# Two tile lists in one block: experts begin on the full tiles of 29 groups

## The reference

```
h = concat(tokens(x) * pos, txt)                        # 128 x 97 x 128
h = h + attn(layernorm(h))     # 8 heads, complex weights, decay mask, gate
h = h + ffn(layernorm(h))

# inside ffn, b*s = 12416 tokens:
o = softmax_attention(x) @ Wo + bo
t = layernorm(x + o) * ln1_g + ln1_b
probs = softmax(t @ gate_W + gate_b)
idx, gw = argmax(probs), max(probs)                     # one of E = 8 experts
hid = gelu(t @ W1[idx] + b1[idx])                       # 128 -> 512
out = (hid @ W2[idx] + b2[idx]) * gw                    # 512 -> 128
```

## Time and profile before

| | |
|---|---|
| median of 3 runs | 1433.87 us (1432.84 to 1434.1) |
| profiled execution | 1432.25 us, of it span 1430.4 |
| PE busy | 1341.3 us (94%), mean granted clock 0.974 |
| DVE busy | 1008.9 us (71%) |
| ACT busy | 723.4 us (51%) |
| POOL busy | 411.4 us (29%) |
| HBM | read 101.27 MB, written 20.82 MB |

### The profile page before, as it was taken

The page is one execution under the profiler, slowest core; times in us unless marked ns, Lnnn a source line. Parts: engine busy times, 40 slices in busy tenths (PEclk is TensorE's granted clock), DMA queues, the critical chain, the costliest instruction groups (busy, mean ns, idle before and its releaser), DMA issues. The chain is left out here.

```text
span 1430.4 us, 40339 instructions
## 1 busy us (share of the span) xinstructions
PE 1341.3 (94%) x14876; PEld 984.3 (69%) x14877; DVE 1008.9 (71%) x2308; ACT 723.4 (51%) x1630; POOL 411.4 (29%) x268
## 2 busy tenths in 40 slices
PE   6889999999999999999999999999999861999996
PEld 5457666666666666666666666666665550999996
DVE  1477777777777777777777777777778643566664
ACT  2135555555555555555555555555555451556654
POOL 0000222222222222222222222222222224466665
PEclk9999999999999999999999999999999895999999
DMA  7522322232222222322233333333310002333331
GB/s 296 216 73 72 83 83 82 83 83 83 83 83 83 83 83 82 83 83 83 83 86 89 93 88 86 88 95 84 85 42 15 18 14 54 104 104 102 102 100 53
DMA packets 94839, 124.57 MB, mean 87 GB/s; under 512 B 56587, under 2 KB 77117, under 8 KB 94176
## 3 DMA queue, kind: packets, MB, share of 16 engines
q1 hardware_dynamic: 38112, 102.47, 22.7%
q0 software_dynamic: 56576, 19.93, 6.7%
HBM read 101.27 MB, written 20.82 MB: 85 GB/s over the span
## 5 line engine op out<-in xcount | busy, mean ns | idle before, releaser
L1126 POOL DMA_INDIRECT expert_rows<-row_sb,placei x128 | 275.7, 2154 | 618.9 <-DVE z L922 566.9
L359 PE MATMUL bank_emb<-x_sb,wtok 128*128 128x256 f32 (+1 forms) x1216 | 323.5, 393 | 4.4 <-DMA x_sb<-in_x_main 3.4
L359 PEld LDWEIGHTS bank_emb<-x_sb,wtok 128*128 128x128 f32 (+1 forms) x1216 | 220.8, 191 | 104.0 <-issue 50.8
L862 DVE TENSOR_TENSOR sm<-bank_s,con 97x776 f32<-97x776 f32 x256 | 240.1, 959 | 26.1 <-PE bank_s L413 13.8
L876 DVE TENSOR_REDUCE mx<-bank_s 97x8 f32<-97x776 f32 x128 | 120.4, 961 | 57.9 <-PE bank_s L479 57.7
L1297 POOL DMA_INDIRECT out_tokens<-yo,tok x104 | 126.1, 1213 | 90.9 <-issue 55.0
L413 PE MATMUL bank_s<-qm,xn 32*97 32x452 f32 x1024 | 133.3, 583 | 4.3 <-DVE prob L881 2.2
L881 DVE TENSOR_TENSOR prob<-bank_s,mx 97x776 f32<-97x776 f32 x128 | 120.7, 964 | 3.3
L731 ACT ACTIVATE prob<-prob 97x776 f32<-97x776 f32 x128 | 108.4, 847 | 26.5 <-DVE prob L881 26.5
L1227 PE MATMUL bank_s<-w2e,hid 128*128 x832 | 109.7, 275 | 0.0
L869 DVE COPY vp<-bank_s 97x128 f32<-97x128 f32 x256 | 70.3, 286 | 55.6 <-PE bank_s L413 55.4
(11 more groups left out here) (181 smaller groups left out, 2330.1 us busy)
## 6 DMA issues: line engine op xcount, KB each, us to landing
x_sb<-in_x_main SPq DMA_DIRECT2D x96, 768.0 KB, 7.2
row<-expert_rows SPq DMA_DIRECT2D x104, 129.0 KB
w1e<-in_exp_w SPq DMA_DIRECT2D x1, 2576.0 KB, 11.7
txt<-in_txt_t SPq DMA_DIRECT2D x32, 64.0 KB, 2.3
w2e<-in_exp_w SPq DMA_DIRECT2D x1, 2048.0 KB, 16.9
expert_rows<-row_sb,placei POOLq DMA_INDIRECT x128, 7.9
out_tokens<-yo,tok POOLq DMA_INDIRECT x104, 2.5
x_sb<-in_x_tail SPq DMA_DIRECT2D x32, 48.0 KB, 2.5
```

Of the source, the lines that this page charges most:

```text
L359: mm = pe.matmul(banks["emb"][:, 0:NPG], wtok[0:k, c, :], x_sb[0:k, c, :], start=(c == 0), stop=(c == KC - 1))
L862: ins = dve.tensor_tensor(sm[:, k % 2, 2 * h:2 * h + 2, :], pair(h), decay, ALU.mult)
L1126: pool.indirect_dma_start(out=rows[:, :], out_offset=bass.IndirectOffsetOnAxis(ap=placei[:, k, c:c + 1], axis=0), in_=row_sb[:, k, c, E:E ...
```

## The change

There is one block instead of two. The list is made in two parts:

- The first has 80 tiles (`NT1`, turns 0 to 9). It is made from `run_k`, a copy of the counts after 29 groups (`KF`), by rounding down, so that it holds full tiles alone. DVE runs it at the end of round 31, PE's product and DVE's copy into `tab` come at the end of round 32. What each expert gave to it is kept in `taken`.
- The second has the other 24 tiles. DVE makes it from the final counts in small pieces, one after each slot of turns 0 and 1; PE's product (in bank s3) and the copy come after turn 1.

SP loads tiles as soon as the scatters of 29 groups have landed, x is used up and the first list is there. The eight blank stores stand between the loads of turns 2 and 3. Before tile 80 SP waits for all scatters, the blanks and the second list. POOL starts on the output scatters right after stage one's last. `w1b` and `row` lie where `x_sb` and `wtok` were (`home_x`), `hid`, `t_t` and `y` where `sm` and `prob` were (`home_s`). `run_i` is made inside `run_on` of the last group. PE waits for five banks to be drained and for the expert weights before its first tile. ACT has turn 0 written out and loops over the rest, PE and DVE have two loops. The steps of stage two (`tile_t`, `hidden`, `output`, `tile_in`, `result`) are unchanged. In the diff, `first_list` and `second_list` are cut to their ends; their middles are the chain of before, the second with `yield` between its steps.

```diff
+TURNS1 = 10
+NT1 = TURNS1 * SLOTS
+KF = next(k for k in range(NG) if -(-(k * N - E * (P - 1)) // P) >= NT1)
+LISTED = KF - 1 + 3 + 1
...
+        home_x = sb("home_x", [P, KC * NPG + KC * P])
+        home_s = sb("home_s", [P, 64 * S])
+
+        def view(home, a, d1, d2, n=P):
+            return home[0:n, a:a + d1 * d2].rearrange("p (a b) -> p a b", a=d1)
+
+        x_sb = view(home_x, 0, KC, NPG)
+        wtok = view(home_x, KC * NPG, KC, P)
+        w1b = view(home_x, 0, SLOTS, PACK)
+        row = view(home_x, SLOTS * PACK, SLOTS, ROW)
+        sm = home_s[0:S, 0:32 * S].rearrange("p (a b c) -> p a b c", a=2, b=4)
+        prob = home_s[0:S, 32 * S:64 * S].rearrange("p (a b c) -> p a b c", a=2, b=4)
+        hid = home_s[:, 0:SLOTS * FF].rearrange("p (s f n) -> p s f n", s=SLOTS, f=FB)
+        t_t = view(home_s, SLOTS * FF, SLOTS, P)
+        y = view(home_s, SLOTS * FF + SLOTS * P, SLOTS, P)
+        yo = sb("yo", [P, SLOTS, P])
+        tok = sb("tok", [P, SLOTS, 1], I32)
...
+        def scattered(eng, n):
+
+            for k in range(ROWS):
+                eng.wait_ge(s_scat[k], 16 * G * len(range(k, n, ROWS)))
...
+            def load(n, s):
+                if later(n):
+                    sp.wait_ge(s_yo, SLOTS * n + s + 1 - SLOTS)
+                first = sp.value_load(tab[0:1, 0, bass.ds(SLOTS * n + s, 1)], min_val=0, max_val=E * REG)
+                sp.dma_start(row[:, s, :], rows[bass.ds(first, P), :]).then_inc(s_row[s], 16)
+
+            def clear(e):
                 first = sp.value_load(run_i[0:1, e:e + 1], min_val=e * REG, max_val=e * REG + B * S)
                 sp.dma_start(rows[bass.ds(first, P), :], blank[:]).then_inc(s_blank, 16)
+
+            for k in range(4):
+                sp.wait_ge(s_xused[k], NG)
+            scattered(sp, KF)
+            sp.wait_ge(s_list, 1)
+            for s in range(SLOTS):
+                load(0, s)
+            for s in range(SLOTS):
+                load(1, s)
+            sp.wait_ge(s_run, 1)
+            for n in range(2, 4):
+                for s in range(SLOTS):
+                    load(n, s)
+                    if s % 2:
+                        clear((n - 2) * 4 + s // 2)
+            with sp.Fori(4, TURNS1) as n:
+                for s in range(SLOTS):
+                    load(n, s)
+            scattered(sp, NG)
+            sp.wait_ge(s_blankin, 32)
+            sp.wait_ge(s_blank, 16 * E)
+            sp.wait_ge(s_list, 2)
+            with sp.Fori(TURNS1, TURNS) as n:
+                for s in range(SLOTS):
+                    load(n, s)
+            for s in range(SLOTS):
+                sp.wait_ge(s_out[s], 16 * TURNS)
...
+            def first_list():
+                pe.wait_ge(s_tokens, NG)
+                pe.wait_ge(s_spread, 1)
+                pe.matmul(banks["emb"][:, 0:2 * NT1], const("ones"), spread[:, :, 0:NT1],
+                          start=True, stop=True).then_inc(s_tabm, 1)
+
+            def second_list():
+                free(pe, "s3")
+                pe.wait_ge(s_spread, 2)
+                pe.matmul(banks["s3"][:, 0:2 * (NT - NT1)], const("ones"), spread[:, :, NT1:NT],
+                          start=True, stop=True).then_inc(s_tabm, 1)
 
...
+                if i == LISTED:
+                    first_list()
...
+            pe.wait_ge(s_list, 1)
+            pe.wait_ge(s_ew, 32)
+            for bank in ("z", "x", "y", "s0", "s1"):
+                free(pe, bank)
+            tile_t(0, 0)
+            tile_t(0, 1)
+            hidden(0, 0)
+            turn(0)
+            turn(1)
+            second_list()
+            with pe.Fori(2, TURNS1) as n:
+                turn(n)
+            pe.wait_ge(s_list, 2)
+            with pe.Fori(TURNS1, TURNS - 1) as n:
+                turn(n)
+            turn(TURNS - 1, True)
 
 
...
+            act.preload_act_table(ACT.Gelu_apprx_tanh)
...
+                if g == KF:
+                    dve.wait_ge(s_runk, 1)
...
+                if g == KF - 1:
+                    read(dve, g, "C.rank")
+                    dve.tensor_copy(run_k[:], run[:]).then_inc(s_runk, 1)
+                if g == NG - 1:
+                    read(dve, g, "C.rank")
+                    dve.tensor_copy(run_i[:], run[:]).then_inc(s_run, 1)
...
+            def first_list():
+                dve.wait_ge(s_runk, 1)
+                made(dve.tensor_tensor(cnt_f[:], run_k[:], const("run0"), ALU.subtract))
+                past_step()
+                made(dve.tensor_copy(cnt_i[:], cnt_f[:]))
+                past_step()
+                made(dve.tensor_scalar(cnt_i[:], cnt_i[:], 7, None, ALU.arith_shift_right))
+                past_step()
...
+                made(dve.tensor_scalar(taken[:], last[:], float(NT1), None, ALU.min))
+                past_step()
+                made(dve.tensor_scalar(upto[:], from_[:], float(NT1), None, ALU.min))
+                made(dve.tensor_scalar(mine[:], from_[:], const("row"), None, ALU.is_le))
+                made(dve.tensor_reduce(tcol[:, 0:1], past[:], AX.X, ALU.add))
+                past_step()
+                made(dve.tensor_tensor(taken[:], taken[:], upto[:], ALU.subtract))
+                made(dve.tensor_tensor(mine[:], mine[:], past[:], ALU.subtract))
+                made(dve.tensor_scalar(from_[:], from_[:], const("row"), -float(P), ALU.subtract, ALU.mult))
+                past_step()
+                made(dve.tensor_tensor(first_row[:], from_[:], const("run0"), ALU.add))
+                past_step()
+                made(dve.tensor_tensor(first_row[:], first_row[:], mine[:], ALU.mult))
+                past_step()
+                made(dve.tensor_reduce(tcol[:, 1:2], first_row[:], AX.X, ALU.add))
+                past_step()
+                made(dve.tensor_scalar(spread[:, 0, 0:NT1], const("ident")[:, 0:NT1], tcol[:, 1:2], None, ALU.mult))
+                past_step()
+                dve.tensor_scalar(spread[:, 1, 0:NT1], const("ident")[:, 0:NT1], tcol[:, 0:1], None,
+                                  ALU.mult).then_inc(s_spread, 1)
+
+            def first_list_copy():
+                dve.wait_ge(s_tabm, 1)
+                dve.tensor_copy(tab[:, :, 0:NT1],
+                                banks["emb"][:, 0:2 * NT1].rearrange("p (k j) -> p k j", k=2)).then_inc(s_list, 1)
...
+            def second_list():
+                n2 = NT - NT1
+                made(dve.tensor_tensor(cnt_f[:], run[:], const("run0"), ALU.subtract))
+                yield
+                past_step()
+                made(dve.tensor_scalar(cnt_i[:], cnt_f[:], float(P - 1), None, ALU.add))
...
+                made(dve.tensor_tensor(tcol[:, 1:2], tcol[:, 1:2], tcol[:, 2:3], ALU.add))
+                yield
+                past_step()
+                made(dve.tensor_scalar(spread[:, 0, NT1:NT], const("ident")[:, 0:n2], tcol[:, 1:2], None, ALU.mult))
+                past_step()
+                dve.tensor_scalar(spread[:, 1, NT1:NT], const("ident")[:, 0:n2], tcol[:, 3:4], None,
+                                  ALU.mult).then_inc(s_spread, 1)
+
+            def second_list_copy():
+                dve.wait_ge(s_tabm, 2)
+                dve.tensor_copy(tab[:, :, NT1:NT], banks["s3"][:, 0:2 * (NT - NT1)].rearrange(
+                    "p (k j) -> p k j", k=2)).then_inc(s_list, 1)
...
                 at(place_sum, i - 3)
                 at(gate_one, i)
...
+                if i == LISTED - 1:
+                    first_list()
+                if i == LISTED:
+                    first_list_copy()
...
+            def turn(n, last=False, beside=None):
+                for s in range(SLOTS):
+                    if not last or s + 2 < SLOTS:
+                        tile_in(*following(n, s, 2))
+                    if s or later(n):
+                        result(*following(n, s, -1))
+                    if beside:
+                        next(beside, None)
+
+            dve.wait_ge(s_list, 1)
+            dve.wait_ge(s_ew, 32)
+            tile_in(0, 0)
+            tile_in(0, 1)
+            second = second_list()
+            turn(0, beside=second)
+            turn(1, beside=second)
+            second_list_copy()
+            with dve.Fori(2, TURNS1 - 1) as n:
+                turn(n)
+            dve.wait_ge(s_list, 2)
+            with dve.Fori(TURNS1 - 1, TURNS - 1) as n:
+                turn(n)
+            turn(TURNS - 1, True)
+            result(TURNS - 1, SLOTS - 1)
 
...
             for i in range(FIRST, LAST):
                 at(scatter, i - 4)
                 at(text, i + 1)
-            pool.wait_ge(s_blankin, 32)
-            pool.wait_ge(s_blank, 16 * E)
-            for k in range(ROWS):
-                pool.wait_ge(s_scat[k], 16 * G * len(range(k, NG, ROWS)))
-            pool.wait_ge(s_ew, 32)
...
+            with pool.Fori(0, TURNS) as n:
```

More of the change, by code:

```diff
@@ L132, in fusion @@
     with ExitStack() as ctx:
[L133 to L155, removed]
         def sb(name, shape, dt=F32):
@@ L213, in place_tokens @@
         mx = sb("mx", [S, 2, 4, 4])
```

(37 more changed lines are left out.)

257 lines of the change are left out of this document (99 added, 158 removed).

## The result

| | before | after |
|---|---|---|
| median | 1433.98 us (1432.84 to 1434.88, 4 runs) | 1419.24 us (1417.72 to 1420.48, 4 runs) |
| profiled execution | 1432.25, span 1430.4 | 1419.48, span 1417.7 |
| PE busy, mean clock | 1341.3 us, 0.974 | 1348.5 us, 0.977 |
| HBM read, written | 101.27 MB, 20.82 MB | 101.27 MB, 20.82 MB |

A forecast was written before the change was run, and what follows sets the result against it. Bound: two dense PE stages with a thin seam of list, scatter drain and block boundary. 1432.25 - 23.5 + 3.3 + 1.0 + 0.5 = 1413.55 us, 1415.2 on the median's scale; range 1411 to 1421.

The forecast's parts named there:

- The seam's gain: Between the stages: first `hidden` product starts at 1195.5 instead of 1218.99, no longer waiting for the last scatter; 23.5 us gained.
- The first list: On DVE after `gate_one(31)`: delays the end of stage one by its full length, 3.3 us, bounds 2.5 and 6.0.
- The half-clock stretch: PE at clock 0.50 late in stage one: only Rival B had it grow over more of group 31, by 3 us.
- Rival B: End of stage one: the list costs its old 6.0 and PE's cold stretch grows by 3; 1421 us, chance 0.12.
- the sum is made against its own time: Whole kernel: terms were added to the profiled execution's 1432.25, giving 1413.55; the difference of -18.7 was then put on the median.
- The collision: First tiles of stage two: `w1b` copies blocked by group 31's scatter on POOL cost 1.0 us, bounds 0 to 3.0.
- Rival A: First tiles: each `w1b` copy and second-list step waits for another POOL piece; 6 us instead of 1.0, 1420.2, chance 0.15.
- The second list: Turns 0 and 1: DVE pieces hidden in idle time; PE's product and a loop entry cost 0.5 us, bounds 0.2 and 1.5.
- Row loads "14 us ahead": Stage two: SP's row loads run 14 us ahead, so the blank stores between them cost nothing, at most 0.8 us.
- the rule's letter: DVE copies beside POOL's scatter: any overlap blocks, and the time would be that of Rival A, 6 us instead of 1.0.
- the likeliest case: Whole kernel: the forecast of 1415.2 us, chance 0.67, with its own range 1412 to 1418.
- the marks set: Prediction wrong if stage one ends over 5 us later, first `hidden` to end grows over 4, or the period changes.

The follow-up runs named there:

- e1: The changed kernel with the first list moved from the end of round 31 into DVE's wait before `y_normal` in round 32; 1421.49 us, ratio 0.986 to before.
- e6: The changed kernel, unchanged, run again in another set; 1428.45 us, ratio 0.9904 to before.
- e10: The kernel before with products of constants, results unused, in PE's waits of rounds 32 to 34; 1424.86 us, ratio 0.9916 to before.
- e11: The program of e8 run again, unchanged, in the set of e9 and e10; 1403.96 us, ratio 0.9782 to before.
- e5: The kernel before, unchanged, run again in another set; 1443.32 us (one execution).
- e9: The program of e8 plus own storage for seven row loads of turn 1, so they wait for no turn 0 result; 1403.1 us, ratio 0.9771 to before.
- e4: The changed kernel plus 23 unused products of constants in PE's waits of rounds 33, 34 and before the first `hidden`; 1421.8 us, ratio 0.9851 to before.
- e8: The changed kernel with the first list in DVE's wait before `y_normal` and 29 unused PE products, rounds 32 to first `hidden`; 1414.58 us, ratio 0.9808 to before.

## Why the prediction was right, and where it fell short

- *The seam's gain, 23.5:* right, 23.04 measured. Inside it the register load ahead of the first `t_t` copy is 0.96 from the end of `place_index` (1201.30 to 1202.26), where 0.5 was estimated in bounds of 0.2 to 1.4; the push by the `run_i` copy is 0.16 instead of 0.23, and 1.04 from there to `hidden` instead of 1.02. The first `hidden` comes 2.0 after `place_index`, where 1.5 was to show the step.
- *The first list, 3.3:* right, 3.34, unstretched and all of it on the path. e1 shows the second half of that: in the hole the same chain, even 1.2 longer for a scatter, costs the list column nothing. The prediction's rows show the idle of 5.39 behind the list, and it did not use it.
- *The half-clock stretch:* the failed term. Rival B had it grow by 3 us as a consequence of the list. Round 33 grew by 4.15, but the list isn't needed for that: before's own length there is 22.55 or 27.37. The step that failed is "the sum is made against its own time": the profiled execution of before had the short form, that of after the long one. What part of the median gain this takes isn't settled; between medians of one set (14.7; 13.4 in e6's, 1441.85 - 1428.45) it is part of both sides. With PE kept warm on both sides it goes away: e10 to e11 is 1424.86 - 1403.96 = 20.9 us. By the sum of the columns it is 23.5 gained in the handoff, 1.2 lost before it (the list, which no longer fits its hole) and 0.6 after it, 21.7.
- *The collision, 1.0 in bounds of 0 to 3:* three blocked copies within the first five, as laid out, and tile 8 is 1.4 late. Part of this is PE's clock, not the copies: before was itself 0.9 later from tile 3 on, in e5 and in e10, than in the first profile. Rival A's cascade didn't come: two steps of the second list lie in after's scatter and took 0.15 and 0.17. The blocking that it named is there, though: in e11 one such step, 0.59 after a POOL piece, took 1.53.
- *The second list, 0.5 in bounds of 0.2 to 1.5:* 0.8 at the end of turn 1. Of this the product is 0.32. The rest seems to be the 0.78 of issue where DVE's loop starts, which the idle 0.62 of other tiles no longer covers, as DVE had just waited for the product; no run takes it away by itself. The loop entry had been put at 0.1. The second loop's entry (tile 80) cost nothing. A further 0.35 at tiles 90 to 92 (0.1 in e11) stays open.
- *Row loads "14 us ahead":* true from turn 2 on, wrong for turn 1, whose loads wait for turn 0's results and then took 6.37 us beside the scatters' traffic. Missing in the sum: 0.35 here, and a wait of 1.13 in e11. In e9, where these loads don't wait for turn 0, PE's wait is gone.
- *The blocking itself:* the Trainium skill (SBUF — State Buffer, section Who interferes with whom) has whoever comes first hold the port pair to its end. The stretched copies agree. The copy at 1202.75, which began 0.11 into a POOL piece and took 0.49, doesn't, nor did `mine` in the earlier trace rows; the measurement decides. In this term the forecast that used the free head (1.0) came nearer to the 1.4 at tile 8 than the rule's letter (6), although the whole time, 1419.24, lies nearer to the 1420.2 of rival A: that is chance, made by other terms.
- *The verdict and the range* hold: 1419.24 lies in 1411 to 1421, but outside the likeliest case's own 1412 to 1418. The range held because it had been drawn wide enough for rivals A and B, not because the 4.15 of round 33 had been foreseen. Of the marks set, one tripped: stage one ended 7.35 us later, over the 5 named, for the reason above. Stage two grew by 2.99, under 4, and the period kept.

## What to carry to other kernels

A serial chain that moves ahead of a boundary costs its whole length where it lands on the path, so look for the hole first: here one began some 10 us further on, and it shrank once PE was faster. Before a few microseconds are ascribed to an edit, look at the granted clock of the same stretch in a second execution of the unchanged kernel. Where an engine's thin rounds drop its clock, useless products in its waits gave 11.7 us, nearly as much as the change. And when a start is pulled forward, recheck every transfer that had slack at the old place.

## What was not expected of the hardware

- The fall to 1.2 GHz after a thin stretch ended after some 7 us in one execution of before and hadn't ended 20 us later in another (round 33: 22.55 or 27.37 us). The first tiles show it too: before took 211.41 or 212.40 us from the first `hidden` to the end.
- A row load of 128 rows took 6.37 us while scatters were landing. In before's seam, after the scatters had landed, one took 2.12 (both from the chain of waits).
- DVE and ACT stood still together for some 3 us in e4 and e8, with no releaser in the profile, and not in e11, the same program as e8. Stage two is 3.0 us apart in these two.
- A `w1b` copy of 0.49 us takes 0.49 if it starts 0.11 after a POOL DMA instruction, and 1.88 if it starts 0.56 after it. A small shift of DVE against POOL is worth 1.4 us.
